# Two stacked cross-attention and mixture layers on one core: from a loop over batches to stages over all four batches

## The reference, cut to what matters

```
x: 4 x 256 x 128 tokens, ctx: 4 x 512 x 128
layer 0: q = LN(x Wq), k = LN(ctx Wk) per head of 8, v = ctx Wv; 16 heads
         x += tanh(g) * (softmax(q k / sqrt(8)) v Wproj + b)
         (x enters through a plain LN of x)
         x += tanh(g) * top-2-of-8 LoRA mixture of a SiLU feed-forward part (128 -> 512 -> 128)
layer 1: c = LN(ctx); l = LN(LN(x)); keys and values from [c, l] (768 tokens), queries from l
         16 heads of 64; x += tanh(g) * (softmax(q k / 8) v Wout)
         x += tanh(g) * top-1-of-8 feed-forward part with GELU (128 -> 512 -> 128)
```

## Time and profile before

| | us |
|---|---|
| median of 3 timed runs (lowest, highest) | 976.95 (976.1, 977.69) |
| the profiled execution | 978.69 |
| its span, first to last instruction | 976.5 |
| mean granted TensorE clock | 0.928 of 2.4 GHz |

### The profile page before, as it was taken

How to read it: one execution, slowest core, us unless ns; L and a number is a source line. 1 busy time by engine, 2 the same in 40 slices (tenths; PEclk the granted TensorE clock), 3 DMA queues, 4 the chain that set the end, 5 groups by cost and what they waited for, 6 DMA issues and landing times.

```text
span 976.5 us, 16529 instructions
## 1 busy us (share of the span) xinstructions
PE 831.4 (85%) x6096; PEld 596.8 (61%) x6096; DVE 629.7 (64%) x1149; ACT 380.5 (39%) x677; POOL 307.1 (31%) x271
## 2 busy tenths in 40 slices
PE   3698969997979778999788976999888977899957
PEld 2555756665855556666575665666576556666646
DVE  6774556847976475774897465585599737455543
ACT  2454244341346425333325532534233642434220
POOL 5131025561513013464312101546341301155431
PEclk8699989998989898999798988999989999799979
DMA  7300000003000000001200000000300000000120
GB/s 176 115 2 17 1 0 2 1 1 87 1 8 2 17 1 1 2 1 40 48 3 8 1 17 0 2 1 1 88 0 7 1 1 1 1 2 1 31 56 6
DMA packets 37783, 18.32 MB, mean 19 GB/s; under 512 B 11432, under 2 KB 36408, under 8 KB 37568
## 3 DMA queue, kind: packets, MB, share of 16 engines
q1 hardware_dynamic: 37696, 17.16, 6.9%
HBM read 16.63 MB, written 0.52 MB: 18 GB/s over the span
## 4 chain that ended last, share of the span: by engine, by line
PE 61%; DVE 25%; issue 8%; ACT 3%; POOL 1%; DMA 1%; SPq 1%; DVEq 0%; ACTq 0%; POOLq 0%
PE ps L1248 58%; DVE max_cols L1143 3%; PE ps L1270 2%; DVE rs_t L810 2%; DVE xn L829 1%; DVE area_k L922 1%; DVE area_k L923 1%; DVE area_p L1223 1%; DVE area_p L1231 1%; DVE cn L829 1%; DVE rs_y L816 1%; DVE area_p L1228 1%; DVE area_k L930 1%; PE ps L1344 1%; ACT area_p L718 1%
## 5 line engine op out<-in xcount | busy, mean ns | idle before, releaser
L718 ACT ACTIVATE area_p<-ps 128x512 f32<-128x512 f32 x192 | 104.2, 595 | 157.9 <-PE ps L1248 157.8
L1143 DVE TENSOR_REDUCE max_cols<-ps 128x2 bf16<-128x1536 f32 x64 | 112.8, 1763 | 67.0 <-PE ps L1248 64.1
L553 POOL TENSOR_TENSOR area_p<-area_p 128x512 f32<-128x512 f32 x64 | 80.4, 1278 | 144.0 <-ACT area_p L718 144.0
L1248 PE MATMUL ps<-q_h,keys 64*128 64x256 f32 x768 | 110.7, 326 | 2.2 <-ACT max_row L585 1.6
L1248 PE MATMUL ps<-area_p,area_v 128*64 128x256 f32 x768 | 108.0, 394 | 0.0
L1248 PE MATMUL ps<-area_v 96*128 96x256 bf16 (+1 forms) x384 | 98.1, 323 | 4.2 <-DVE rowmax L994 2.8
L994 DVE TENSOR_REDUCE rowmax<-ps 128x2 f32<-128x1024 f32 x64 | 77.8, 1223 | 25.9 <-PE ps L1248 24.1
L529 POOL TENSOR_TENSOR diag<-negidentb,rowmax 128x256 bf16<-128x256 bf16 x64 | 39.2, 613 | 162.6 <-DVE rowmax L994 158.5
L585 ACT ACTIVATE area_v<-ps 96x768 bf16<-96x768 bf16 (+1 forms) x64 | 53.7, 892 | 88.3 <-PE ps L1248 50.5
L637 ACT ACTIVATE area_p<-ps 128x512 f32<-128x512 f32 x128 | 69.7, 595 | 46.6 <-PE ps L1248 46.3
L1248 PEld LDWEIGHTS ps<-q_h,keys 64*128 64x128 f32 x768 | 74.0, 188 | 22.3 <-issue 9.2
(11 more groups left out here) (234 smaller groups left out, 1625.4 us busy)
## 6 DMA issues: line engine op xcount, KB each, us to landing
area_v<-in_L_ffn_W_dram SPq DMA_DIRECT2D x16, 512.0 KB, 6.3
w<-in_L_ffn_W_dram SPq DMA_DIRECT2D x1, 2048.0 KB
ctx_in<-in_ctx_dram SPq DMA_DIRECT2D x4, 256.0 KB, 2.8
area_p<-in_L_xattn_Wkv_dram SPq DMA_DIRECT2D x1, 1024.0 KB, 7.5
area_v<-in_L_ffn_B_dram SPq DMA_DIRECT2D x9, 64.0 KB
x_in<-in_x_dram SPq DMA_DIRECT2D x4, 128.0 KB, 2.2
area_p<-in_L_xattn_Wq_dram SPq DMA_DIRECT2D x1, 512.0 KB, 8.3
wout<-in_L_xattn_Wout_dram SPq DMA_DIRECT2D x1, 512.0 KB
```

What stands on the lines that cost most here:

```text
L553: pool.tensor_tensor(psum_1[:, p % 2, j, :], p1[:, (6 * p + j) % PR1, :], p1[:, (6 * p + 2 + j) % PR1, :], ALU.add).then_inc(g_part.sem, 1)
L718: act.activation(p1[:, n % PR1, :], bank(SCORE_BANK[u][j]), ACT.Exp, scale=SCALE1).then_inc(a_exp1.sem, 1)
L1143: dve.tensor_reduce(max_cols[:, p % 2, :, j * D1], bank(0, 3).rearrange("p (t k) -> p t k", t=TQ), AX, ALU.max).then_inc(d_max1.sem, 1)
L1248: return pe.matmul(o, lhsT, rhs, start=start, stop=stop)
```

## The change

The loop over batches is gone. Every engine's list is written out in five stages, each over all four batches: preparation of layer 0's keys, queries and values; the first attention in 16 quads of heads; the first feed-forward part, with batch i+1's routing put between batch i's products; the second attention in one run of 32 pairs (g = 8 b + p); the routed part, again with the next batch's routing woven in. In preparation the norms of keys and queries are taken in the transposed layout, with a centring matrix folded into the weights, squares summed by small products and factors spread by transposes; the bf16 parts are written to memory and read back as stacks by DMA (`stacked`, 3 writes and 12 or 13 reads a batch), and a quad's maxima row is put into the stack by a DMA too (`maxima_row`), so that a head's scores are four products of 73 rows. The first attention's maxima are fp32r products of 32 rows, reduced 512 wide, eight a quad.

In the second attention the keys, latent keys and queries of pair g+3 are projected inside iteration g, in two halves, through bank 7, which value inputs, output products and turned contexts also pass (`X_USES`); other value inputs pass bank 5. Maxima come in three parts for both heads side by side, in banks 4 and 5, reduced 1024 wide, with a small maximum over the parts. Exponentials are 128x1024. GpSimd adds three parts and folds them, so that the sums are one product a head. Numerator and denominator have bank 6 alone. All value products of pair g-1 stand behind the last scores of pair g.

```diff
+            for g in range(G1 + 1):
+                b, p = divmod(g, NPAIR)
+                if g < G1:
+                    if g + 1 < G1:
+                        max1(g + 1, 2)
+                    scores1(g, 0)
+                    scores1(g, 1)
+                    if g + 1 < G1:
+                        max_row_in(g + 1)
+                        if 1 <= p <= 4:
+                            values_in(b, 1, p - 1)
+                        if p >= 5 and b + 1 < B:
+                            values_in(b + 1, 0, p - 5)
+                    if g + 3 < G1:
+                        project(g + 3, 0)
+                if g < G1:
+                    scores1(g, 2)
+                    if g + 2 < G1:
+                        max1(g + 2, 0)
+                    if g + 3 < G1:
+                        project(g + 3, 1)
+                if g >= 1:
+                    values1(g - 1, (0, 1, 2, 3))
+                    values1(g - 1, (4, 5))
+                    sums1(g - 1)
+                if g < G1:
+                    if g + 2 < G1:
+                        max1(g + 2, 1)
...
+            def max1(g, part):
...
+                elif part == 1:
+                    pe.wait_ge(d_max1.sem, d_max1.after(g, 1))
+                elif part == 2:
+                    pe.wait_ge(d_max1.sem, d_max1.after(g, 2))
```

VectorE's list of the same loop, and the waits of its division:

```diff
+            def divide1(g):
+                dve.wait_ge(e_den1.sem, g + 1)
...
+                then(dve.reciprocal(o1[:, g % OS, :], bank(6)[:, NQ:2 * NQ]))
+                dve.tensor_tensor(o1[:, g % OS, :], bank(6)[:, 0:NQ], o1[:, g % OS, :],
+                                  ALU.mult).then_inc(d_o1.sem, 1)
...
+            for g in range(G1):
+                b, p = divmod(g, NPAIR)
+                if g + 1 < G1:
+                    row_max1(g + 1, 2)
+                if g + 3 < G1:
+                    proj_low(g + 3, 0)
+                if g + 2 < G1:
+                    row_max1(g + 2, 0)
+                if g + 3 < G1:
+                    proj_low(g + 3, 1)
+                if g >= 1:
+                    divide1(g - 1)
+                if g + 2 < G1:
+                    row_max1(g + 2, 1)
...
+                if b + 1 < B:
+                    if p == 0:
+                        context_stats(b + 1)
+                    if p == 1:
+                        context_scale(b + 1)
+                    if p == 2:
+                        context_norm(b + 1)
+                        latents_norm(b + 1)
+                    if p == 3:
+                        context_turned(b + 1)
+                    if p == 4:
+                        latents_turned(b + 1)
```

The first attention, its DMAs and the two pipelined parts on TensorE and VectorE:

```diff
+            stacked(0)
+            stacked(1)
+            maxima_row(0)
+            maxima_row(1)
+            stacked(2)
+            stacked(3)
+            for q in range(2, AQ):
+                maxima_row(q)
...
+            def rows0(q):
+                pe.wait_ge(d_max0.sem, d_max0.after(q, 8))
...
+            for i in range(B):
+                lora0(i)
+                if i + 1 < B:
+                    head0(i + 1)
+                down0(i)
+                if i + 1 < B:
+                    common0(i + 1)
...
+            for i in range(B):
+                hidden0(i)
+                if i + 1 < B:
+                    route0(i + 1)
+                if i + 2 < B:
+                    norm_b(i + 2)
+                down0(i)
+                if i + 1 < B:
+                    lora0(i + 1)
+                residual_b(i)
...
+                if i + 1 < B:
+                    masks1(i + 1)
+                if i + 2 < B:
+                    norm_d(i + 2)
+                select1(i, 1, 0)
+                if i + 1 < B:
+                    masked(i + 1, 0)
+                    masked(i + 1, 1)
```

More of the change, by code:

```diff
@@ L757, in batch, with bias_out @@
+            def bias_out(i):
+                act.wait_ge(e_b2.sem, i + 1)
+                if i >= 1:
+                    act.wait_ge(d_y.sem, d_y.after(i, 0))
+                copy(sel[:, :, E, :], bank(7)[:, 0:NQ].rearrange("p (t d) -> p t d", t=TQ)).then_inc(a_b2.sem, 1)
+            routed(0)
+            softmax(0)
+            for c in range(FC):
+                w2_high(c)
+            mask_out(0)
+            bias_out(0)
+            for i in range(B):
                 for n in range(2):
-                    act.wait_ge(e_pre1.sem, e_pre1.after(b, n + 1))
@@ new lines, in scale0 @@
+            def scale0(b):
+                k = b % 2
+                dve.wait_ge(e_var.sem, b + 1)
+                vh, y, tmp = (a[:, :] for a in rs_wide)
+                own()
+                then(dve.tensor_scalar(vh, bank(3 * k + 1)[:, 0:TK * H], EPS, -0.5, ALU.add, ALU.mult))
+                if b >= 2:
+                    dve.wait_ge(e_rb.sem, e_rb.after(b - 2, 2))
+                rsqrt(vh, y, tmp, columns=False,
+                      last=rexp[:, k, :, :].rearrange("p t (h d) -> p (t h) d", h=H)).then_inc(d_rs.sem, 1)
@@ new lines, in residual0 @@
+            def residual0(b):
+                x = x_of(b)
+                then(dve.scalar_tensor_tensor(out=x, in0=wide(bproj0[:, :], TQ, P), scalar=G_X0, in1=x,
+                                              op0=ALU.mult, op1=ALU.add))
+                dve.wait_ge(e_proj.sem, b + 1)
+                dve.scalar_tensor_tensor(out=x, in0=halves(bank(7)[:, 0:NQ]), scalar=G_X0, in1=x, op0=ALU.mult,
+                                         op1=ALU.add).then_inc(d_xA.sem, 1)
+            for q in range(2):
+                for n in range(8):
+                    row_max0(q, n)
@@ L1168, in batch @@
-                if not last:
-                    context_low_ahead(b + 1)
-                divide(NPAIR - 2)
-                divide(NPAIR - 1)
-                then(dve.memset(probT, 0.0))
-                dve.wait_ge(e_y1.sem, e_y1.after(b, 2))
-                dve.scalar_tensor_tensor(out=xr[:, :, :], in0=bank(1)[:, 0:NQ].rearrange("p (t d) -> p t d", t=TQ),
-                                         scalar=G_X1, in1=xr[:, :, :], op0=ALU.mult,
-                                         op1=ALU.add).then_inc(d_x.sem, 1)
@@ new lines, in use_before, with max_row_in @@
+            def use_before(use, g):
+                b, half, t = use
+                if (b, half) == (0, 0):
+                    return True
+                at = NPAIR * b + t + 1 if half else NPAIR * (b - 1) + t + 5
+                return at <= g
+            def max_row_in(g):
+                pe.wait_ge(d_max1.sem, d_max1.after(g, 4))
+                for t in range(TQ):
+                    ins = mm(tok(bank(4), t), max_cols[:, g % 2, t, :], negidentb[:, :])
+                ins.then_inc(e_mrow.sem, 1)
```

2503 lines of the change are left out of this document (1325 added, 1178 removed).

## The result

The changed kernel takes 1092.45 us (median of four runs, 1092.18 to 1092.68) where the kernel before, on the same chip, takes 977.24: a ratio of 1.118 (95% interval 1.116 to 1.120), 115 us slower. The span of its profiled execution is 1090.9 us. I had forecast 1026.5 in a range of 980 to 1085: the direction was right, the size 66 us short.

A forecast was written before the change was run, and what follows sets the result against it. The prediction took the second attention's chain through VectorE's division as the bound. First attention 243.5, first feed-forward 107.5, second attention 513 and routed part 162 sum to 1026, with 0.45 added 1026.5 us; range 980 to 1085.

The forecast's parts named there:

- The bound of the second attention: Second attention: chain sums, division, reduction delays the next maxima; 13.8 us a pair against 9.6, stage 513 us; chance 0.72.
- The shares of the clock (15 us) and of the norms (28): Second attention's loop: 15 us for a few clock drops, 28 us for next batches' norms on VectorE delaying maxima.
- Rival 1, pipelining in full: Stages outside the second attention go by their busiest engine: 943 us; wins if those parts come under 463; chance 0.12.
- Rival 2, the clock down in every pair: Second attention: clock drops in every pair, 29 x 3.2 us in place of 15, 1104 us; chance 0.11, whole or in good part.
- A quad at 8.2 us: First attention: a quad of four heads takes 8.2 us, about 1 of it waiting for VectorE's reductions; 14 such quads.
- Products with 32 rows: Unpriced cost: such products run from four at once (quad 7 us) to none overlapping.
- costs not shown: Row DMAs behind stacks, 32-row products and GpSimd masked copies; together -25 to +30 us.
- turns and tail: First attention: three turns 4.5 us and the tail 6, added to 14 quads; stage ends at 243.5.
- The third quad at 118: First attention: third quad waits until 118 us for its maxima row, issued behind two batches' stacks, 26 issues at about 0.5.
- The routed part, 162: Last stage: entry 33.5 us, three batches of 36.5, and a last 19.5: 162 us, before 4 x 52.
- the feed-forward part: First feed-forward stage: entry 13.5 us, three periods of 25.2, last 18.5: 107.5 us, before 4 x 40.
- The range: Whole kernel: 980 to 1085 us, leaving out rival 1 and the upper part of rival 2.

The follow-up runs named there:

- Kernel 3: Changed kernel with second maxima ahead among the value products on TensorE, and VectorE's division a step later, behind the next third reduction: 1010.0 us.
- kernel 1: Changed kernel with one swap on VectorE: second reduction of pair g+2's maxima in front of the division of pair g-1: 1094.4 us.
- kernel 4: Kernel 3 with the next batch's norms cut into five pieces, one a pair, begun two pairs earlier: 992.65 us.
- kernel 6: Changed kernel with the first attention's maxima products over all 128 rows in place of 32 (another result): 1056.6 us.
- kernel 7: Changed kernel with eight unread 128x128 products before the last wait for a quad's maxima row: 1076.1, 1079.6, 1082.9 and 1095.2 us.
- Kernel 9: Changed kernel with SyncE reordered: third and fourth batch's stack writes ahead of the reads, third quad's maxima row between the two batches' reads: 1072.8 us.
- Kernel 10: Changed kernel with the routed part's entry reordered: second batch's norm behind first batch's masked inputs, down-weight split behind first masks' copies: 1087.5 us.

## Why the prediction was right and wrong

**The bound of the second attention: right.** The chain from the sums through the division was seen in the two lists of instructions, and 13.8 us a pair was set against 13.1 to 14.6 measured; TensorE's wait was 2.1 us in the mean where I had said about 3; the loop took 472 for 477, with its entry 512 for 513. Kernel 3 shows the cause. That the sum came out so near is partly luck: a pair at full clock takes 13.1, some 20 us less over 28 pairs, and what the rows have beyond 13.1 is 58 us from the third distance on, where the forecast had 43 for norms and clock. What the forecast missed inside it is that a second wait, for the maxima row, stood behind the first: it appeared in kernel 1 and cancelled the gain. The shares of the clock (15 us) and of the norms (28) were not tested one by one; kernel 4 gives back 17 of the latter.

**Rival 1, pipelining in full: fell.** The stages outside the second attention took 579 us and not under 463.

**Rival 2, the clock down in every pair: fell, though by less than I said.** The stage's clock is 0.89 from 443 to 915.4. TensorE waits 26 times for 2.1 us or more for the reduction; the 2.5 us behind such a wait ran at 1.00 nine times and lower 17 times, 2.12 us at 654.15 with full clock behind it and 2.13 at 667.26 with 0.50. But a drop lengthens a pair by 1.4 us (14.5 for 13.1) and not by 3.2: some 24 us by estimate (17 times 1.4), for my 15 and the rival's 93. The Trainium skill (TensorE: Matmul & The Clock Gate, "HAM oscillation — how this bites in real kernels") tells of a kernel that waits for a DMA before each tile and starts every one at the low clock; in these shorter waits for a reduction it is borne out by part of the pairs only.

**A quad at 8.2 us: the step that failed.** The mechanism of the quad was right at full clock: 7.6 us in kernel 6, 7.9 in the good quads of kernel 7. The term was mis-sized by the clock: twelve steps from 140.89 to 273.99 are 11.1 us each. I had priced the clock only in the second attention and the routed part, from the one place where I had seen it fall. For the first attention I foresaw the wait of each quad ("about 1" for VectorE's reductions) and gave it no price in clock, nor did I ask how much of the array the products around it fill. "Products with 32 rows" stood among the costs not shown, but as a matter of overlap (four at once, or none), and not of the clock. Kernel 6 takes 36 us back with the rows alone, more than the stage's net error of 27, since turns and tail were put too high. Why products of 32 rows go with the low clock, and full rows behind a longer wait don't, is not shown.

**The third quad at 118: mis-sized by 21 us.** The queue was named as the cause, and its steps read otherwise than I had summed. The third batch's writes begin 5 us later than the 90 of the sum, at 94.97, behind the second row. The two sets of writes and their returns take 3.9 and 9.2 us, together what the forecast left for them. But the 26 issues behind them take 23.0 us (98.84 to 110.6 and 119.79 to 131.0), 0.9 each where I had about 0.5: 10 us more. And the row behind them takes 7.8 us from issue to scores (131.09 to 138.90), where the earlier trace rows gave 2.65: 5 us more. Kernel 9 gives 20 back by order alone. The bound under "Costs not shown", up to the 28 us of the third quad once more, held this.

**The routed part, 162 for 175.5.** VectorE's small operations beside GpSimd were priced from the earlier trace rows for the second attention, and not looked for in this entry, where GpSimd's longest split stands beside a norm. Kernel 10 gives 10.1 of the 13.5 back in its profiled execution. The 4 us of the feed-forward part were not followed up.

**The range** reached 1085. It took the bound of each unknown cost once and none for a clock below 1.00 in a busy stage; that one term, 36 us on the upper end, would have put 1092 inside.

## What to carry to other kernels

Follow each engine's list over the border of an iteration: an instruction that waits for the last step of this iteration must not stand in front of one that the next iteration's first step waits for, and after mending it look for the next wait in the same list (kernel 1 turned 44 us of waits into 59 of another, kernel 3 removed 58). A stage of products with 32 rows should be costed at the low clock as well as the full one, as here, and of a queue ask how long the issues themselves take and what lands last, not only what is issued last. Pipelining over batches paid here only once these orders were mended: nearly the same instructions in another order went from 1092 to 964 us, against 977 before.

## What was not expected of the hardware

- The granted clock was 0.50 in stretches where TensorE was busy 3.00 of 3.00 us, with maxima products of 32 rows and value products of 32 columns among them, and 1.00 at 6.44 of 7.60 with 128 rows in the maxima products.
- The same quad of 69 products took 7.9 us at 1.00 or 12.8 at 0.55 in one execution, behind the same wait of 0.27 us.
- Behind a wait of 2.1 us TensorE ran on at 1.00 in some pairs of the second attention and at 0.50 in others.
- Products in four different quarters of the columns overlap: 32 in 1.93 us, against 32 in 7.17 over all columns, both at full clock.
- A VectorE operation of two columns took 2.3 us beside a GpSimd pass of 2.3, for 0.16 alone; one of four columns took 1.80 in kernel 3 (0.18 alone).
- DMAs issued behind the reads of a stack landed 7.8 to 11.5 us after their issue, and 26 of these issues took 23.0 us.
